# Order of transposes and one-hot products in the attention edge pass

## The chip, the cores and the metric

The program runs on one core of one Trainium2 chip. The metric is the device time of one execution in microseconds. The kernel before took 4116.12 us in the median of three runs (4115.34 to 4116.28).

## The reference, cut to what matters

Two graph attention layers over 3125 nodes and 100,000 edges sorted by target, then a sum over neighbours and three dense layers, each part closed by a layer norm:

```python
def gatv2_layer(x, src, dst, Wl, Wr, att, bias, n_nodes, heads):
    xl = (x @ Wl).reshape(N, heads, Dh)
    xr = (x @ Wr).reshape(N, heads, Dh)
    e = leaky_relu(xl[src] + xr[dst], 0.2)
    logits = einsum('ehd,hd->eh', e, att)
    m = segment_max(logits, dst)
    a = exp(logits - m[dst])
    alpha = a / segment_sum(a, dst)[dst]
    out = segment_sum(alpha[:, :, None] * xl[src], dst)
    return out.mean(axis=1) + bias
```

The first layer has 8 heads, the second 4; a head has 64 features.

## The kernel before, in words

The edges are laid out in 900 units of 125 edges (`T`). A chunk is 20 units, so there are 45 chunks a layer (`NCH`); a chunk is worked in five turns `q` of four units each (`Q`). `edge_pass` (line 753) is one pass over the 45 chunks; it runs once for each attention layer, so there are 450 turns.

For its four units a turn needs a matrix of 128 rows and 500 columns: rows 0 to 63 are the features of the source nodes, rows 64 to 127 those of the target nodes, one column for each edge. `turn(c, q)` (line 876) makes it in one PSUM bank, `ps_x`:

- Four transposes (line 887), one a unit: `xs` holds the gathered source rows, 125 edges by 64 features in float32, and the identity is the moving operand. They write PSUM partitions 0 to 63.
- Four products (line 890), one a unit: a bfloat16 table `xw` of the window's node features (96 by 64) against a one-hot matrix `oht` (96 by 125). They write PSUM partitions 64 to 127. The last one counts up the semaphore `x_ready`, on which ScalarE waits to copy the bank to SBUF (`copy_xT`, line 988), to be used by TensorE one turn later.

TensorE's order is written out by hand in `body` (line 959), chunk by chunk and turn by turn: `turn`; then four parts in which the projection of the turn before (`project`, line 900, 500 moving columns in float32, all 128 rows and columns of the array; four in layer 1, two in layer 2) alternates with the weighted sums of a unit three chunks back (`sums`, line 951); then `reduce` of three turns back (lines 909 and 912), whose small matmuls write four strips of 32 PSUM partitions; and in turns 0, 1 and 2 a group of full-array transposes and matmuls to `ps_t` (lines 922, 930 to 933, 940). So the turns 1, 2 and 3 start behind such a full-array group, the turns 0 and 4 behind `reduce`. A float32 matmul that is no transpose stands as two instructions in the profile (line 900 has x2 where one is written), a transpose as one.

GpSimd gathers the source rows, one indirect DMA for each unit (line 825), into a ring of 6 chunks in layer 1 and 9 in layer 2, and may refill a chunk's tile when `sums` has used it (`v_ready`, line 822). TensorE waits for a chunk's 20 gathers at its turn 0 (line 879).

Of the kernel before, what the change touches and what calls it, by code (L numbers as in the profile page):

```python
# [14 lines left out]
N, D, E = 3125, 64, 100000  # L15
# [3 lines left out]
T = 125  # L19
# [3 lines left out]
Q = 4  # L23
# [20 lines left out]
NQ = 5  # L44
# [123 lines left out]
def sbuf(nc, ctx, name, shape, dt=F32):  # L168
    return ctx.enter_context(nc.sbuf_tensor(name, shape, dt))
# [583 lines left out]
def edge_pass(nc, k, lay):  # L753
# [12 lines left out]
    with ExitStack() as ctx:  # L766
        ph, nm = "e_", lay.nm + "e_"
        dlb = [sbuf(nc, ctx, f"{nm}dlb{r}", [3 * WN, CU * T], BF16) for r in range(3)]
        oht = [sbuf(nc, ctx, f"{nm}oht{r}", [3 * WN, CU * T], BF16) for r in range(2)]
# [30 lines left out]
        xs, gath = lay.xs, lay.gath  # L800
        xw, wins, ld_x, ld_w = lay.xw, lay.wins, lay.ld_x, lay.ld_w
# [15 lines left out]
        with nc.Block() as block:  # L817
# [57 lines left out]
            def _(pe):  # L875
                def turn(c, q):
                    r = c.slot(XR)
                    if q == 0:
                        pe.wait_ge(gath[r], c.uses(XR) * GB)
                        pe.wait_ge(ld_x[c.slot(3)], c.uses(3) * 16 * CU)  # L880
                        pe.wait_ge(s["oht_ready"], c.val(1, 1))
                    if c.after(1) or q >= 2:
                        pe.wait_ge(s["xT_ready"], c.val(NQ, q - 1))
                    ps = ps_x[(c.slot(2) * NQ + q) % 2]
                    for j in range(Q):
                        n = j * NQ + q
                        pe.transpose(ps[0:D, j * T:(j + 1) * T], xs[r][:, n, 0:D], k.ident[0:T, 0:T])  # L887
                    for j in range(Q):
                        n = j * NQ + q
                        ins = pe.matmul(ps[D:128, j * T:(j + 1) * T], xw[c.slot(3)][:, n, :],  # L890
                                        oht[c.slot(2)][:, n * T:(n + 1) * T], start=True, stop=True)
                    ins.then_inc(s["x_ready"], 1)

                def project(c, q, part):
# [64 lines left out]
                def body(c, q):  # L959
                    if c.there():  # L960
                        turn(c, q)
                    zc, zq = lag(c, q, 1)
                    bc, bq = lag(c, q, 15)
                    rc, rq = lag(c, q, 3)
                    for part in range(4):
                        if part % (4 // C) == 0 and (c.after(1) or q >= 1) and zc.there():
                            project(zc, zq, part // (4 // C))
                        if c.after(3) and bc.there():
                            sums(bc, bq, part)
                    if (c.after(1) or q >= 3) and rc.there():  # L970
                        reduce(rc, rq)
                    b = c.back(2)
                    if c.after(2) and b.there():
                        if q == 0:
                            maxima_out(b)
                        if q == 1:
                            fifth_out(b)
                        if q == 2:
                            weights_out(b)
# [1076 lines left out]
```

## Time and profile before

| | |
|---|---|
| median of three runs | 4116.12 us |
| profiled execution, its own time | 4112.72 us |
| its span on the chip | 4110.9 us |
| TensorE (PE) busy | 3302.8 us, 80% |
| GpSimd (POOL) busy | 2883.6 us, 70% |
| VectorE (DVE) busy | 2788.8 us, 68% |
| ScalarE (ACT) busy | 1702.9 us, 41% |
| mean granted clock of TensorE | 0.896 |

In the profile L900 is line 900 of the kernel; PE is a matmul, PEld the weight load ahead of it. The edge pass of layer 1 lies at about 190 to 1790 us, that of layer 2 at about 2110 to 3470 us. Ends of matmuls are modelled, so the start times say more than the busy times: the time from the start of one matmul to the start of the next is what a matmul costs in a stream. A group that stands in one row as x4 gives its first start and the time to its modelled last end; the start of its last matmul is that end less the duration of one.

### The profile page before, as it was taken

How to read it: one execution, taken by the hardware profiler on the slowest of the kernel's cores; microseconds unless marked ns; L12 is line 12 of the kernel's file. 1: busy time of each engine (PE TensorE's matmuls, PEld its weight loads, DVE VectorE, ACT ScalarE, POOL GpSimd, SP SyncE). 2: the span in 40 equal slices, each digit the busy share in tenths (PEclk: the TensorE clock that was granted, in tenths of full speed). 3: DMA queues.
4: the chain of work that ended last, by engine and by line, in shares of the span. 5: the costliest groups of instructions: out<-in, count | busy, mean ns of one | idle time of the engine just before them, and what ended most of it. 6: DMA issues, size and time to landing. Idle time of an engine off the chain costs nothing. (4 is left out here: it accounts for less than half of the span.)

```text
span 4110.9 us, 76192 instructions
## 1 busy us (share of the span) xinstructions
PE 3302.8 (80%) x24219; PEld 2216.7 (54%) x24219; DVE 2788.8 (68%) x6704; ACT 1702.9 (41%) x3682; POOL 2883.6 (70%) x2229
## 2 busy tenths in 40 slices
PE   0499999999999999986259977777777778457886
PEld 0246666666666666664226645554555546345663
DVE  3558888888888888875527855556555666378872
ACT  3254444444444444412215433333333332156651
POOL 4488888887777777434778888888888883567860
PEclk9999999999999999966679988888888887589897
DMA  2233334343333333222124433333333332112120
GB/s 57 51 67 86 84 83 87 85 87 85 87 84 87 85 85 81 68 59 65 49 42 84 92 67 68 73 67 69 67 72 70 68 68 45 35 34 47 40 46 28
DMA packets 612700, 277.98 MB, mean 68 GB/s; under 512 B 450601, under 2 KB 572877, under 8 KB 611716
## 3 DMA queue, kind: packets, MB, share of 16 engines
q1 hardware_dynamic: 263920, 103.06, 11.5%
q0 software_dynamic: 110784, 80.17, 11.1%
q10 hardware_dynamic: 237600, 89.88, 9.0%
q8 instruction: 198, 3.24, 0.3%
q14 instruction: 198, 1.62, 0.1%
HBM read 164.01 MB, written 106.40 MB: 66 GB/s over the span
## 5 line engine op out<-in xcount | busy, mean ns | idle before, releaser
L900 PE MATMUL L_e_ps_z<-L_e_xT,L_w_abs 128*128 128x500 f32 x2700 | 1496.6, 640 | 0.0
L825 POOL DMA_INDIRECT L_e_xs<-in_x_dram,src_idx x880 | 1185.3, 1347 | 343.9 <-issue 261.0
L825 POOL DMA_INDIRECT L_e_xs<-x_d,src_idx x820 | 1071.2, 1306 | 253.3 <-issue 249.8
L951 PEld LDWEIGHTS L_e_ps_v<-L_e_xs,L_e_p 125*128 125x128 f32 x5400 | 857.2, 203 | 628.1 <-issue 571.6
L995 ACT ACTIVATE L_e_rl<-L_e_ps_z 128x500 f32<-128x500 f32 x1350 | 793.0, 587 | 877.8 <-PE L_e_ps_z L900 877.8
L951 PE MATMUL L_e_ps_v<-L_e_xs,L_e_p 125*128 125x65 f32 x5400 | 793.9, 274 | 12.1 <-DVE L_e_acc L1179 10.4
L1179 DVE SCALAR_TENSOR_TENSOR L_e_acc<-L_e_acc,L_e_row,L_e_ps_v 128x130 f32<-128x130 f32 (+1 forms) x1440 | 448.3, 311 | 426.7 <-PE L_e_ps_v L951 283.1
L887 PE MATMUL L_e_ps_x<-ident,L_e_xs 125*64 125x125 f32 x1800 | 288.1, 285 | 301.5 <-DMA L_e_xs<-x_d,src_idx 245.2
L988 ACT ACTIVATE L_e_xT<-L_e_ps_x 128x500 f32<-128x500 f32 x450 | 264.2, 587 | 610.5 <-PE L_e_ps_x L890 603.8
L900 PEld LDWEIGHTS L_e_ps_z<-L_e_xT,L_w_abs 128*128 128x128 f32 x2700 | 425.7, 197 | 76.2 <-issue 22.4
L1162 DVE TENSOR_TENSOR L_e_p<-L_e_ohc,L_e_ae 125x640 f32<-125x640 f32 x540 | 427.1, 818 | 0.0
L1652 POOL DMA_INDIRECT g_xs<-x_d,src_idx x240 | 295.8, 1233 | 132.9 <-issue 72.5
L887 PEld LDWEIGHTS L_e_ps_x<-ident,L_e_xs 125*64 125x64 f32 x1800 | 188.6, 119 | 345.1 <-DMA L_e_xs<-x_d,src_idx 254.4
L1184 DVE SCALAR_TENSOR_TENSOR L_e_acc<-L_e_acc,L_e_keep,L_e_ps_v 128x65 f32<-128x65 f32 x540 | 134.9, 277 | 304.4 <-PE L_e_ps_v L951 302.3
L1090 DVE SCALAR_TENSOR_TENSOR L_e_f<-L_e_rl,L_sign 128x500 f32<-128x500 f32 x450 | 326.1, 725 | 21.1 <-ACT L_e_rl L995 20.9
L1090 DVE SCALAR_TENSOR_TENSOR L_e_f<-L_e_rl,L_sign,L_e_f 128x500 f32<-128x500 f32 x450 | 330.1, 734 | 4.1 <-ACT L_e_rl L995 0.6
L1768 ACT ACTIVATE g_cnt<-g_ps_c 125x400 bf16<-125x400 f32 x480 | 241.6, 504 | 127.9 <-PE g_ps_c L1703 122.1
L1799 DVE TENSOR_SCALAR g_ohk<-t_keys_n,t_key_of 125x200 bf16<-125x200 bf16 x960 | 225.6, 330 | 7.5 <-PE g_ps_c L1703 7.1
L909 PE MATMUL L_e_ps_l<-L_e_xT,L_w_lin 128*32 128x125 f32 x3600 | 190.3, 283 | 14.1 <-DVE L_e_f L1090 14.1
L1703 PE MATMUL g_ps_c<-g_ohk,g_ohr 125*128 125x200 bf16 x960 | 169.6, 264 | 36.6 <-DVE g_ohk L1799 34.3
L1713 PE MATMUL g_ps_s<-g_x,g_cnt 125*128 125x192 bf16 x1500 | 194.7, 258 | 0.2 <-DVE g_sums L1805 0.2
L890 PE MATMUL L_e_ps_x<-L_e_oht,L_e_xw 96*64 96x125 bf16 x1800 | 192.8, 232 | 0.0
(304 smaller groups left out, 3661.0 us busy)
## 6 DMA issues: line engine op xcount, KB each, us to landing
L_v_d<-L_e_acc ACTq DMA_DIRECT2D x225, 260.0 KB
L_e_dlb<-dloc_d SPq DMA_DIRECT2D x90, 468.8 KB
L_v_d<-L_e_acc ACTq DMA_DIRECT2D x225, 130.0 KB
L_e_xw<-x_d SPq DMA_DIRECT2D x1800, 12.0 KB
L_e_xs<-in_x_dram,src_idx POOLq DMA_INDIRECT x900
L_e_xs<-x_d,src_idx POOLq DMA_INDIRECT x900
L_e_lim<-limits_d SPq DMA_DIRECT2D x180, 39.1 KB
g_xs<-x_d,src_idx POOLq DMA_INDIRECT x240, 3.0
```

The costliest lines, as they stand in the source:

```text
L825: pool.indirect_dma_start(xs[c.slot(XR)][:, n, 0:D], None, lay.x_rows, bass.IndirectOffsetOnAxis(k.src_idx[:, u:u + 1], 0)).then_inc(gath[ ...
L887: pe.transpose(ps[0:D, j * T:(j + 1) * T], xs[r][:, n, 0:D], k.ident[0:T, 0:T])
L900: pe.matmul(ps_z[part % ZR][:, 0:QT], lay.w_abs[:, part * 128:(part + 1) * 128], xT[q][:], start=True, stop=True).then_inc(s["z_ready"], 1)
L951: ins = pe.matmul(ps_v[u // 2 % 2][:, u % 2 * VX + v * XW:u % 2 * VX + (v + 1) * XW], p[st % 3][:, u % NQ, v, :, :].rearrange("e n h -> e ...
L988: act.activation(xT[q][:], ps_x[(c.slot(2) * NQ + q) % 2][:, 0:QT], ACT.Copy).then_inc(s["xT_ready"], 1)
L995: act.activation(rl[n % NE][:], ps_z[part % ZR][:, 0:QT], ACT.Relu, scale=1.0 - SLOPE).then_inc(s["relu_done"], 1)
L1090: dve.scalar_tensor_tensor(out=f[g % 3][:], in0=rl[(C * g + part) % NE][:], scalar=lay.sign[:, part:part + 1], in1=rl[(C * g) % NE][:] if ...
L1162: ins = dve.tensor_tensor(p[n % 3][:, :, v, :, :], ohc[c.slot(2)][:, us, :].unsqueeze(3).to_broadcast([T, NQ, WN, HL]), ae[c.slot(2)][:, u ...
L1179: ins = dve.scalar_tensor_tensor(out=to, in0=prev, scalar=row[c.slot(2)][:, u:u + 1], in1=ps_v[u // 2 % 2][:, u % 2 * VX:(u % 2 + 1) * VX] ...
L1652: pool.indirect_dma_start(xs[p][:, j, :], None, table, bass.IndirectOffsetOnAxis(k.src_idx[:, u:u + 1], 0)).then_inc(gath[p], 16)
L1768: act.activation(cnt[i % CR][:, :, 2 * j:2 * j + 2, :], ps_c[n % 2][0:T, 0:2 * KEYS].rearrange("r (u t n) -> r t u n", u=2, n=EN), ACT.Cop ...
L1799: dve.tensor_scalar(ohk[v % KR][:], keys_n[:], key_of[:, v:v + 1], None, ALU.is_equal).then_inc(s["hot"], 1)
```

## The change

In `turn`, each unit's product is issued first and its transpose right behind it, through the four units. The operands, the outputs and the number of instructions are the same. The count on `x_ready` moves from the last product to the last transpose, which is now the last instruction.

```diff
                     for j in range(Q):
                         n = j * NQ + q
-                        pe.transpose(ps[0:D, j * T:(j + 1) * T], xs[r][:, n, 0:D], k.ident[0:T, 0:T])
-                    for j in range(Q):
-                        n = j * NQ + q
-                        ins = pe.matmul(ps[D:128, j * T:(j + 1) * T], xw[c.slot(3)][:, n, :],
-                                        oht[c.slot(2)][:, n * T:(n + 1) * T], start=True, stop=True)
+                        pe.matmul(ps[D:128, j * T:(j + 1) * T], xw[c.slot(3)][:, n, :],
+                                  oht[c.slot(2)][:, n * T:(n + 1) * T], start=True, stop=True)
+                        ins = pe.transpose(ps[0:D, j * T:(j + 1) * T], xs[r][:, n, 0:D], k.ident[0:T, 0:T])
                     ins.then_inc(s["x_ready"], 1)
```

## Rows read from the trace of the kernel before

**Rows 1.** The page: busy time by engine, and PE and its clock in 40 slices.

```profile
PE 3302.8 (80%) x24219; PEld 2216.7 (54%) x24219; DVE 2788.8 (68%) x6704; ACT 1702.9 (41%) x3682; POOL 2883.6 (70%) x2229
...
PE   0499999999999999986259977777777778457886
...
PEclk9999999999999999966679988888888887589897
```

**Rows 2.** Busy time of each engine in a stretch of layer 1 and of layer 2.

```profile
core 0: us, PE busy (x) PEld busy (x) DVE busy (x) ACT busy (x) POOL busy (x), PEclk, DMA share, GB/s
300.00:1400.00 1100.00, 1100.00 (x7902) 730.63 (x7894) 918.26 (x1958) 543.21 (x1122) 868.68 (x642) 1.00 0.39 86
2400.00:3400.00 1000.00, 779.30 (x5966) 511.32 (x5965) 579.81 (x1396) 357.75 (x808) 809.99 (x624) 0.87 0.36 69
```

**Rows 3.** Groups of PE instructions, 300 to 1400 us: busy, mean ns, idle before.

```profile
L887 PE MATMUL L_e_ps_x<-ident,L_e_xs 125*64 125x125 f32 x624 | 93.9, 273 | 0.0
```

**Rows 4.** Waits (total us, times, longest): POOL in 900 to 1400 us.

```profile
POOL L_e_xs L825 <- PE L_e_ps_v L951: 39.9, 13, 3.8
```

**Rows 5.** Waits: PE in 190 to 300 us, the start of layer 1.

```profile
PE L_e_ps_x L887 <- DMA L_e_xs<-in_x_dram,src_idx: 6.8, 1, 6.8
```

**Rows 6.** Waits: PE in 2400 to 3400 us, layer 2.

```profile
PE L_e_ps_x L887 <- DMA L_e_xs<-x_d,src_idx: 220.7, 31, 8.2
```

**Rows 7.** PE in order of time (start, us to last end): layer 1, behind a full-array group.

```profile
1000.65 0.70 PE L922 MATMUL L_e_ps_t<-ident,L_e_mx 128*125 128x128 f32 x4
1001.19 0.59 PE L887 MATMUL L_e_ps_x<-ident,L_e_xs 125*64 125x125 f32 x4
1001.71 0.41 PE L890 MATMUL L_e_ps_x<-L_e_oht,L_e_xw 96*64 96x125 bf16 x4
1002.05 1.10 PE L900 MATMUL L_e_ps_z<-L_e_xT,L_w_abs 128*128 128x500 f32 x2
1003.00 0.56 PE L951 MATMUL L_e_ps_v<-L_e_xs,L_e_p 125*128 125x65 f32 x4
1003.39 1.06 PE L900 MATMUL L_e_ps_z<-L_e_xT,L_w_abs 128*128 128x500 f32 x2
1004.28 0.56 PE L951 MATMUL L_e_ps_v<-L_e_xs,L_e_p 125*128 125x65 f32 x4
```

**Rows 8.** The same turn in narrow windows: transposes 2 to 4, transpose 4, product 4.

```profile
1001.30 0.48 PE L887 MATMUL L_e_ps_x<-ident,L_e_xs 125*64 125x125 f32 x3
...
1001.51 0.27 PE L887 MATMUL L_e_ps_x<-ident,L_e_xs 125*64 125x125 f32 x1
...
1001.91 0.22 PE L890 MATMUL L_e_ps_x<-L_e_oht,L_e_xw 96*64 96x125 bf16 x1
```

**Rows 9.** PE in order of time: layer 1, a turn that starts behind `reduce`.

```profile
1022.00 0.42 PE L909 MATMUL L_e_ps_l<-L_e_xT,L_w_lin 128*32 128x125 f32 x8
1022.24 0.40 PE L912 MATMUL L_e_ps_l<-L_e_f,L_sign_sum 128*32 128x125 f32 x8
1022.56 0.62 PE L887 MATMUL L_e_ps_x<-ident,L_e_xs 125*64 125x125 f32 x4
1023.11 0.41 PE L890 MATMUL L_e_ps_x<-L_e_oht,L_e_xw 96*64 96x125 bf16 x4
```

**Rows 10.** PE in order of time: neighbour sums, both on the full array.

```profile
3679.88 0.25 PE L1703 MATMUL g_ps_c<-g_ohk,g_ohr 125*128 125x200 bf16 x1
3679.96 1.02 PE L1731 MATMUL g_ps_w<-g_blk,g_winhot 96*98 96x512 f32 x2
```

**Rows 11.** PE in order of time: merge, full-array transposes, then matmuls to 64 partitions.

```profile
1887.10 0.65 PE L1373 MATMUL L_n_ps_t<-ident,L_n_agg 125*128 125x125 f32 x4
1887.67 1.07 PE L1392 MATMUL L_n_ps_o<-L_n_aggT,L_n_wl 128*64 128x125 f32 x8
```

**Rows 12.** Stretches again: early layer 2, merge, all of layer 1 (columns of Rows 2).

```profile
2190.00:2350.00 160.00, 159.18 (x1369) 105.64 (x1368) 132.43 (x323) 81.67 (x185) 130.10 (x99) 1.00 0.48 91
1880.00:2100.00 220.00, 97.83 (x558) 77.00 (x557) 106.92 (x173) 42.87 (x102) 131.35 (x114) 0.65 0.17 43
262.00:1787.00 1525.00, 1521.92 (x10926) 1007.27 (x10925) 1267.89 (x2698) 754.14 (x1557) 1126.13 (x834) 1.00 0.37 83
```

## The prediction

> **What bounds the kernel now.** I read the page's totals and slices first, then the busy time by stretch, the waits, and last the order of time of single turns. PE is the busiest engine, and its slices say where: nines through layer 1, sevens through most of layer 2 [rows 1]. A busy share is no proof, so the waits decide.
>
> In layer 1 PE is busy for all of the 1100 us looked at, at a granted clock of 1.00 [rows 2], and its transposes there have an idle time before them of 0.0 [rows 3]. It is GpSimd that waits for PE there, to have a tile of the ring back [rows 4]. So PE's own stream sets the time of layer 1, and what a turn gets longer, the layer gets longer. Only at its start does PE wait once for a gather, 6.8 us [rows 5]; that was for chunk 2, so what chunks 0 and 1 lose is taken out of that wait. 43 chunks, 215 turns, count in full.
>
> In layer 2 PE waits 31 times in 1000 us, 220.7 us in all, for the gathers of a chunk, once a chunk [rows 6]. So there GpSimd and its gathers set the time: a chunk takes 1000 / 31 = 32.3 us, of which PE waits 7.1 us. What a chunk of PE's work gets longer is taken from that wait while it stays under 7.1 us. The first ten chunks of layer 2, whose rows were partly gathered ahead, run without waits (PE 159.18 of 160 us busy [rows 12]); time lost there only makes PE reach the waiting part later, with the waits of 35 chunks to make it good.
>
> **What a switch costs.** Call a transpose T, a product P, the first projection Z, the first matmul of the sums V. In the turn of [rows 7, 8]:
>
> - T to T: 1001.30 to 1001.51 in two steps, 0.107 us each.
> - T4 to P1: 1001.51 to 1001.71, 0.20 us. So 0.09 us more than a T takes in its stream.
> - P1 to P4: 1001.71 to 1001.91, 0.20 us, three steps. A P in its stream takes less than 0.06 us; the first step is some 0.08 us, since P1's weights weren't loaded ahead.
> - P4 to Z1: 1001.91 to 1002.05, 0.145 us; again 0.09 us over the 0.055 that P takes.
> - Z1 to V: 0.95 us (1002.05 to 1003.00), where the next pair, whose weights could be loaded ahead during other work, takes 0.89 us (1003.39 to 1004.28).
>
> So twice a turn, between T and P and between P and Z, the stream stops for about 0.09 us, and the matmul behind the stop shows its weight load: 0.025 us for P. For T it is seen in the turn behind `reduce`: T1 to P1 is 0.55 us there [rows 9] against 0.52 us in [rows 7], so 0.03 us.
>
> What makes a switch? Three pairs of rows tell. A bfloat16 matmul followed by a float32 one, both on the full array, has no stop: 0.08 us for 200 columns [rows 10]. So the data type isn't it. The full-array transposes of L922 are followed by our T without one: the last starts at 1001.35 - 0.27 = 1001.08, T1 at 1001.19, 0.11 us [rows 7]. But L912, which writes strips of 32 partitions, followed by T has one: 1022.37 to 1022.56, 0.19 to 0.20 us [rows 9], and so have full-array transposes followed by float32 matmuls into 64 partitions: 1887.48 to 1887.67 [rows 11]. So T goes with the full array though it fills only 64 columns, P goes with the matmuls that use a part of the columns, and each change between the two kinds costs a stop. In the old order a turn has two such changes (T to P, P to Z), and a third before T1 when `reduce` was ahead. In the new order it has eight: into P1, and seven between T and P. T4 to Z1 is none.
>
> The Trainium skill says so as a rule, in "TensorEngine Tiling (Array Packing)", Key Properties: a change of the tiling mode drains TensorE, a change of tile within a mode doesn't; its Gotcha 2 adds that column tiling and the transpose mode for float32 input exclude each other. The trace agrees with both.
>
> **The change part by part.** Nothing is added or removed: the same eight matmuls and weight loads, no DMA, no wait. Only their order, in 450 turns. I sum from the start of the last matmul ahead of the turn to the start of V.
>
> Before: behind `reduce` (turns 0 and 4) 1022.37 to V; with T1 at 0.20, T1 to P1 0.55, P1 to Z1 0.34, Z1 to V 0.94, that is 2.03 us. Behind a full-array group (turns 1 to 3): 1001.08 to 1003.00 = 1.92 us [rows 7, 9].
>
> After, in both kinds of turn:
>
> - into P1: 0.20 us. A stop is due there in every turn. From `reduce` to P the trace has no row; both kinds use a part of the columns, but of another width. Bounds: 0.10 (no stop) to 0.20. I take 0.20, as for every other change of shape seen; by the lower one turns 0 and 4 lose 0.10 less, 9 us over the layer.
> - P to T, four times: 0.145 as from P to Z, and 0.025 of load shown behind the stop: 0.17, together 0.68. No row has P to T. Bounds: 0.055, a P in its stream with no stop, and 0.145 + 0.107 = 0.25, the stop and as much again as a whole T. I take 0.17, the nearest row, since L912 to T is a stop too.
> - T to P, three times: 0.20 + 0.03 of T's own load = 0.23, together 0.69 (0.68 unrounded).
> - T4 to Z1: 0.107 + 0.03 = 0.13 us.
> - Z1 to V: no stop ahead of Z1, so its load runs beside T4. 0.94 less the load that showed, twice the 0.05 by which it exceeds the next pair: 0.84 us.
>
> Sum 0.20 + 0.68 + 0.68 + 0.13 + 0.84 = 2.53 us. Turns 0 and 4 lose 0.50, turns 1 to 3 lose 0.61; mean 0.57 us a turn, 2.8 us a chunk.
>
> Layer 1: 215 x 0.57 = 122 us, all on the path. Layer 2: 2.8 us of the 7.1 us that PE waits a chunk, hidden by the gathers; only the last chunk, behind its last gather, has nothing to hide it: 3 us. If the cover weren't there the layer would pay 225 x 0.57 = 128 us. The clock there is 0.87 and some turns run at the lower level, where a stop may cost more; even at twice the price, 5.7 us, it stays under 7.1.
>
> `x_ready` now comes from T4, whose modelled duration is 0.27 us where that of P4 is 0.22 [rows 8]. ScalarE's copy starts 0.05 us later against its last matmul; the copy is used by Z in the next turn, some 5 us on, so this costs nothing, and 0.05 us a turn (11 us) if that cover were gone. The same count lets SP load and VectorE build the one-hot tiles of chunks ahead, also far off.
>
> Sum: 4112.7 us (the profiled execution) + 122 + 3 = 4238 us. The median of the runs stands 3.4 us above that execution, so 4241 us; I say 4242.
>
> **The rivals.**
>
> *The pairs overlap (faster).* T writes PSUM partitions 0 to 63 and P 64 to 127, different columns of the array. For it: L909's eight matmuls of 125 columns in four strips take from 1022.00 to 1022.24, four side by side in the time of one [rows 9]. If T and P were tiles of one mode, P would lie beside T: 0.20 + 0.03 + 3 x 0.107 + 0.20 + 0.94 = 1.69 us, 0.34 less behind `reduce`, 0.23 less behind a full-array group, mean 0.27; 215 turns give -59 us, 4057 us. Against it: T4 to P1 stops already now, though P's columns are free. The condition from which it decides is that this stop is not the shape but only the first use of the other columns. The Trainium skill's rule that different tiles can load and multiply in parallel (same page, Key Properties) would give this result. Chance 6%. A weaker form, in which stops vanish but nothing overlaps, saves about 0.1 us a turn, some 4090 us; 3%.
>
> *P to T is free.* Stops only on the way into P. Then 4 x 0.115 less: 0.11 us a turn, +24 us, 4140 us. Against it: P to Z and L912 to T both stop. 5%.
>
> *The clock falls or layer 2 loses its cover.* The stops make PE do less in a turn. In the merge, with many stops and waits, the granted clock is 0.65; in early layer 2, with 4.5 us turns and the two stops, it is 1.00 [rows 12]. A new layer 1 turn loses 8 stops of 0.09 in over 7.5 us, nearer to the latter. If layer 1 fell to layer 2's 0.87, between the levels of 1.2 and 2.4 GHz, it would take 1525 / 0.87 - 1525 = 228 us more, 4470 us. If layer 2 lost a third of its cover, some 40 us more, 4280 us. 5% together.
>
> *It makes no difference*, because PE's stream isn't what sets layer 1 after all, 4116 us: against it stands the zero wait. 2%.
>
> **How the numbers follow.** The forecast has 79%, and its own bounds, from the P-to-T bounds and the entry from `reduce`, are 4140 (which is the second rival) to 4310 (0.25 instead of 0.17, four times, 215 turns: +69). I don't give these ends full weight: 4175 to 4290 leaves out the fast rivals, the free P to T and the fallen clock, some 20% with the edges. Within 0.2%, about 8 us, is what can't be told from no change: 3%. Faster 9%, slower 88%.
>
> **What would show it.** In the order of time of a layer 1 turn T and P should stand singly, P to T 0.17 us apart and T to P 0.23, with an idle time in the weight loads before each; Z1 should follow T4 without one. A turn should be 0.5 to 0.6 us longer in layer 1 at a clock of 1.00, GpSimd should wait longer for PE there, and in layer 2 PE should wait some 4 us a chunk where it waits 7, the period of 32.3 us unchanged. I am wrong if T and P start within 0.03 us of each other, if P to T is 0.06, or if layer 2 is longer by over 10 us.

## The result, and the profile after

The changed kernel takes 4258.53 us in the median of four runs, where the kernel before takes 4116.13: a ratio of 1.0345, interval 1.0327 to 1.0363, or 142 us more. The profiled execution took 4257.54 us, with a span of 4255.7 us.

The forecast was 4242 us, slower, by a stop of TensorE's stream at each change between transpose (T) and product (P). That is what the trace shows. First the page, busy time by engine and PE's slices:

```profile
PE 3554.1 (84%) x24219; PEld 2298.5 (54%) x24219; DVE 2794.7 (66%) x6704; ACT 1701.6 (40%) x3682; POOL 2894.6 (68%) x2229
...
PE   0499999999999999996619998888888888557786
```

As many instructions as before, yet PE is "busy" for 251 us more [rows 1]. The modelled durations, 0.24 and 0.30 us in the rows below, reach over the 0.17 and 0.23 us to the next start, the stop included. So a stop counts as busy time, and the busy time says nothing of work.

A turn of layer 1 of the changed kernel, PE in order of time (start, us to the last end; the answer to [rows 7]). Line 887 is now the product and line 889 the transpose; 898 is the projection (its first one is Z1) and 949 the weighted sums (V):

```profile
1002.39 0.40 PE L910 MATMUL L_e_ps_l<-L_e_f,L_sign_sum 128*32 128x125 f32 x8
1002.72 0.70 PE L938 MATMUL L_e_ps_t<-ident,L_e_lg 128*125 128x128 f32 x4
1003.35 0.24 PE L887 MATMUL L_e_ps_x<-L_e_oht,L_e_xw 96*64 96x125 bf16 x1
1003.53 0.30 PE L889 MATMUL L_e_ps_x<-ident,L_e_xs 125*64 125x125 f32 x1
1003.75 0.24 PE L887 MATMUL L_e_ps_x<-L_e_oht,L_e_xw 96*64 96x125 bf16 x1
1003.93 0.30 PE L889 MATMUL L_e_ps_x<-ident,L_e_xs 125*64 125x125 f32 x1
...
1004.56 0.24 PE L887 MATMUL L_e_ps_x<-L_e_oht,L_e_xw 96*64 96x125 bf16 x1
1004.73 0.30 PE L889 MATMUL L_e_ps_x<-ident,L_e_xs 125*64 125x125 f32 x1
1004.87 1.01 PE L898 MATMUL L_e_ps_z<-L_e_xT,L_w_abs 128*128 128x500 f32 x2
1005.71 0.56 PE L949 MATMUL L_e_ps_v<-L_e_xs,L_e_p 125*128 125x65 f32 x4
```

From start to start P to T is 0.17 to 0.18 us, T to P 0.23, T4 to Z1 0.14, Z1 to V 0.84. From the last transpose of the group ahead (1003.42 - 0.27 = 1003.15) to P1 it is 0.20. The sum to V is 2.56 us; 2.53 was forecast, 1.92 was the old.

The busy time by stretch (the answer to [rows 2 and 12]: layer 1, and a stretch of layer 2 as far into it as before), the waits of POOL in 900 to 1400 us, of PE in 190 to 300 us, and of PE in 2500 to 3560 us (the answers to [rows 4 to 6]):

```profile
300.00:1400.00 1100.00, 1100.00 (x7282) 703.07 (x7281) 848.62 (x1804) 501.34 (x1033) 795.55 (x591) 1.00 0.37 79
2530.00:3530.00 1000.00, 851.40 (x5962) 527.46 (x5962) 582.37 (x1402) 357.18 (x808) 812.15 (x617) 0.91 0.35 69
...
262.00:1914.00 1652.00, 1649.22 (x10927) 1050.57 (x10925) 1270.64 (x2697) 754.53 (x1557) 1120.87 (x834) 1.00 0.35 76
```

```profile
POOL L_e_xs L825 <- PE L_e_ps_v L949: 73.7, 13, 5.8
```

```profile
PE L_e_ps_x L887 <- DMA L_e_xs<-in_x_dram,src_idx: 3.1, 1, 3.1
```

```profile
PE L_e_ps_x L887 <- DMA L_e_xs<-x_d,src_idx: 154.5, 31, 6.2
```

In 1100 us of layer 1 PE now gets through 7282 matmuls instead of 7902, still at a clock of 1.00 and still with no wait. GpSimd waits 5.7 us a chunk for PE where it waited 3.1. In layer 2 PE's wait falls from 7.1 to 5.0 us a chunk.

Where the time lies shows in the first and last start of the transposes of each layer (duration min/median/max in ns, then first and last start in us), before and after:

```profile
L887 PE MATMUL L_e_ps_x<-ident,L_e_xs x900: 267/270/417, 198.8 to 1766.1; 125*64 125x125 f32 x180
L887 PE MATMUL L_e_ps_x<-ident,L_e_xs x900: 267/270/418, 2112.8 to 3448.1; 125*64 125x125 f32 x180
```

```profile
L889 PE MATMUL L_e_ps_x<-ident,L_e_xs x900: 295/297/418, 198.7 to 1893.9; 125*64 125x125 f32 x180
L889 PE MATMUL L_e_ps_x<-ident,L_e_xs x900: 295/297/418, 2240.1 to 3593.0; 125*64 125x125 f32 x180
```

Layer 1 is 1695.2 us long instead of 1567.3, 127.9 more. The start of layer 2 moves by 127.3 us, its last transpose by 144.9: layer 2 is 17.6 us longer, where 3 were forecast.

So two questions are left for experiments. Is it the change of array shape that costs, and not the mix of types or the order? And where do the 15 us in layer 2 come from that the forecast doesn't have?

### The profile page after: what moved, and what is told of

The parts are those of the page before. It is cut to its first block and busy times, and to the rows that moved or that the text cites. A ratio compares the mean times of both kernels' runs of the same rounds, so it can differ in the third digit from the quotient of the medians.

```text
span 4255.7 us, 76192 instructions
## 1 busy us (share of the span) xinstructions
PE 3554.1 (84%) x24219; PEld 2298.5 (54%) x24219; DVE 2794.7 (66%) x6704; ACT 1701.6 (40%) x3682; POOL 2894.6 (68%) x2229
## 5 line engine op out<-in xcount | busy, mean ns | idle before, releaser
L898 PE MATMUL L_e_ps_z<-L_e_xT,L_w_abs 128*128 128x500 f32 x2700 | 1438.4, 618 | 0.0
L825 POOL DMA_INDIRECT L_e_xs<-x_d,src_idx x820 | 1086.5, 1325 | 253.3 <-issue 249.5
L887 PE MATMUL L_e_ps_x<-L_e_oht,L_e_xw 96*64 96x125 bf16 x1800 | 446.7, 248 | 210.2 <-DMA L_e_xs<-x_d,src_idx 158.8
L889 PE MATMUL L_e_ps_x<-ident,L_e_xs 125*64 125x125 f32 x1800 | 551.9, 307 | 0.0
L898 PEld LDWEIGHTS L_e_ps_z<-L_e_xT,L_w_abs 128*128 128x128 f32 x2700 | 438.2, 202 | 33.2 <-issue 16.8
L887 PEld LDWEIGHTS L_e_ps_x<-L_e_oht,L_e_xw 96*64 96x64 bf16 x1800 | 193.9, 108 | 444.7 <-DMA L_e_xs<-x_d,src_idx 167.3
L889 PEld LDWEIGHTS L_e_ps_x<-ident,L_e_xs 125*64 125x64 f32 x1800 | 200.1, 111 | 126.9
```

The costliest lines, as they stand in the source:

```text
L825: pool.indirect_dma_start(xs[c.slot(XR)][:, n, 0:D], None, lay.x_rows, bass.IndirectOffsetOnAxis(k.src_idx[:, u:u + 1], 0)).then_inc(gath[ ...
L889: ins = pe.transpose(ps[0:D, j * T:(j + 1) * T], xs[r][:, n, 0:D], k.ident[0:T, 0:T])
L898: pe.matmul(ps_z[part % ZR][:, 0:QT], lay.w_abs[:, part * 128:(part + 1) * 128], xT[q][:], start=True, stop=True).then_inc(s["z_ready"], 1)
```

## The experiments

Twelve runs, in three groups of four, each group on another chip and with its own runs of the kernel before. These took 4147, 4121 and 4113 us, so each run is held against its own group. The first group has no trace of the kernel before. "Layer 1" and "layer 2" below are spans between the first and the last projection (line 900, 898 in the changed kernel) of a layer in the profiled execution, and are held against the first profile; there the kernel before has 1575.1 and 1338.6 us, the changed one 1701.2 and 1353.8.

**Products first.** Four products, then four transposes.

```diff
-  T0 T1 T2 T3 P0 P1 P2 P3
+  P0 P1 P2 P3 T0 T1 T2 T3
```

> The four products of a turn first, then its four transposes; all else as in the kernel before. Theory S (each change between matmuls that use a part of the columns and those on the full array stops the stream for 0.09 us, and the next weight load shows): changes per turn go from 2 (3 behind reduce) to 2 (1 behind reduce, if strips of 32 to 64 columns is no change). Sum from the last matmul ahead to V: 0.20 + 0.20 + 0.145 + 0.35 + 0.11 + 0.84 = 1.85 us against 2.03 and 1.92, mean -0.12 us a turn, layer 1 -26 us, about 4090 us. Rival A (it is the nearness of products and transposes, or the product going first, that costs): no gain or slower, 4116 us or more.

Measured: ratio 0.9903, interval 0.9871 to 0.9934, or -41 us where -26 were expected. In order of time, layer 1:

```profile
1002.99 0.70 PE L940 MATMUL L_e_ps_t<-ident,L_e_lg 128*125 128x128 f32 x4
1003.62 0.41 PE L888 MATMUL L_e_ps_x<-L_e_oht,L_e_xw 96*64 96x125 bf16 x4
1003.96 0.62 PE L891 MATMUL L_e_ps_x<-ident,L_e_xs 125*64 125x125 f32 x4
1004.41 1.01 PE L900 MATMUL L_e_ps_z<-L_e_xT,L_w_abs 128*128 128x500 f32 x2
1005.26 0.56 PE L951 MATMUL L_e_ps_v<-L_e_xs,L_e_p 125*128 125x65 f32 x4
```

From the last matmul ahead (1003.69 - 0.27) to V 1.84 us; 1.85 was expected. A chunk takes 34.76 us through most of layer 1, where the kernel before takes 35.39: 0.126 us a turn less, 0.12 expected. Layer 1 is 17 us shorter in the profiled execution; a third of its chunks took about 35.3 us. The kernel before was slow on this chip as well, so the 41 us can't be told apart into order and chip, and the size is taken from the rows. The product going first costs nothing, so that half of Rival A is out. Its other half, that a product next to a transpose costs, is for the next runs.

**Two and two.** P0 P1 T0 T1 P2 P3 T2 T3: four changes.

> Two products, two transposes, two products, two transposes. Theory S: four changes a turn between old 2 and new 8; sum 2.07 us a turn against 2.03 and 1.92, mean +0.10 us, layer 1 +22 us, layer 2 a few us: 4135 to 4145 us. Rival A (a cost for each product that stands next to a transpose): two of the four pairs are neighbours in order, so half of the 142 us, 4187 us.

Measured: ratio 1.0146, interval 1.0103 to 1.0189, that is +61 us, close to the rival and outside the 4135 to 4145 us (19 to 29 more) of the switch theory. But the excess isn't between products and transposes. Ahead of its projections in layer 1 PE had 31.3 us of "issue" waits, where the products-first kernel had 3.4, and VectorE had "remote" waits ahead of its sums, where the kernel waits for the store of an earlier sum; the kernel before had none of these. Waits in 300 to 1700 us:

```profile
PE L_e_ps_z L900 <- issue: 31.3, 29, 4.8
```

```profile
DVE L_e_acc L1184 <- remote: 65.0, 24, 3.9
```

The run was therefore made again in another group.

> Two products, two transposes, twice, once more, because the first run of it was on a chip where VectorE and ScalarE also waited for stores in layer 1. Switch theory: 35.9 us a chunk in layer 1, +22 us there, +20 to +35 us in all with what layer 2 adds. Rival A (half of the full cost): +70 us.

Measured: ratio 1.0041, interval 1.0028 to 1.0055, +17 us. PE has no wait in layer 1 now:

```profile
1004.64 0.30 PE L888 MATMUL L_e_ps_x<-L_e_oht,L_e_xw 96*64 96x125 bf16 x2
1004.87 0.40 PE L891 MATMUL L_e_ps_x<-ident,L_e_xs 125*64 125x125 f32 x2
1005.20 0.30 PE L888 MATMUL L_e_ps_x<-L_e_oht,L_e_xw 96*64 96x125 bf16 x2
1005.43 0.41 PE L891 MATMUL L_e_ps_x<-ident,L_e_xs 125*64 125x125 f32 x2
1005.67 1.01 PE L900 MATMUL L_e_ps_z<-L_e_xT,L_w_abs 128*128 128x500 f32 x2
```

A chunk takes 35.95 us in every chunk from the fourth on (35.9 expected), layer 1 1599.0 us, +24. The total is below the expected 20 to 35 because layer 2 is 12 us shorter than before. Rival A wanted 70, so it is out. The steps between the matmuls are the same in both runs (P to T 0.15 us, T to P 0.20), so the other 44 us of the first run are not the price of this order. They went with the waits shown; why that execution had them is not known.

**Wide products.** The shape is the only thing taken out. The window table is given 128 columns with zeros in the first 64, and the product writes all 128 partitions; the transpose then writes over the lower half. Types, order and the transpose mode stay those of the changed kernel.

```diff
-    lay.xw = [sbuf(nc, ctx, f"{lay.nm}e_xw{r}", [3 * WN, CU, D], BF16) for r in range(3)]
+    lay.xw = [sbuf(nc, ctx, f"{lay.nm}e_xw{r}", [3 * WN, CU, 128], BF16) for r in range(3)]
...
+                    pool.memset(lay.xw[r][:, :, 0:D], 0.0).then_inc(s["ones"], 1)
...
-                        pe.matmul(ps[D:128, j * T:(j + 1) * T], xw[c.slot(3)][:, n, :],
+                        pe.matmul(ps[0:128, j * T:(j + 1) * T], xw[c.slot(3)][:, n, :],
```

> The order of the changed kernel, product then transpose through the four units, but each product on the full array: its stationary operand is 128 columns wide, the first 64 zeros, so it writes zeros to PSUM partitions 0 to 63, which the transpose behind it overwrites. Theory S: no change of shape within a turn, so no stop: layer 1 turns 0.31 us shorter than before, -67 us, about 4050 us. Rival B (the stop comes with the change between bfloat16 product and float32 transpose, whatever columns they use): stays at about 4258 us.

> The same wide products, all four ahead of the four transposes. Theory S: as the wide pairs, about 4050 us, since order no longer matters. Rival B: two stops a turn left, about 4090 us, well below the wide pairs.

Measured: ratios 0.9899 (0.9866 to 0.9931) for the pairs and 0.9885 (0.9841 to 0.9928) with the products first, against a kernel before of 4147 us: 4101 and 4102 us. That is 46 and 44 us less where 67 were expected; Rival B, which had the pairs at 4258, is far off. The pairs were run again:

> The wide products in pairs once more, for its size: layer 1 chunks of 33.9 us where the kernel before has 35.4, less the waits for gathers that now show in layer 1: -45 to -60 us in all, layer 2 within 15 us of the old.

Measured: 4085.52 us, ratio 0.9934, interval 0.9921 to 0.9947, -27 us. In order of time, a turn behind `reduce` that had waited for its gather:

```profile
1006.77 0.23 PE L890 MATMUL L_e_ps_x<-L_e_oht,L_e_xw 96*128 96x125 bf16 x1 [0.96 <-DMA L_e_xs<-in_x_dram,src_idx]
1006.84 0.27 PE L893 MATMUL L_e_ps_x<-ident,L_e_xs 125*64 125x125 f32 x1
1006.95 0.22 PE L890 MATMUL L_e_ps_x<-L_e_oht,L_e_xw 96*128 96x125 bf16 x1
1007.01 0.27 PE L893 MATMUL L_e_ps_x<-ident,L_e_xs 125*64 125x125 f32 x1
...
1007.45 1.00 PE L902 MATMUL L_e_ps_z<-L_e_xT,L_w_abs 128*128 128x500 f32 x2
```

P to T is 0.06 and T to P 0.11 us, in the very order that costs 0.17 and 0.23 when the product fills half the columns. A bfloat16 product next to a float32 transpose is no stop: Rival B is out, and the price belongs to the shape. The edit also moves the product's first PSUM partition from 64 to 0. [rows 11] speak against this being what counts: line 1392 writes 64 partitions from partition 0 on, and a stop stands ahead of it. An undisturbed chunk is 33.89 us (expected 33.9) in pairs and 33.82 with the products first: order no longer matters, within 0.014 us a turn.

The gain is smaller than the expected 45 to 60 us, for two reasons seen in the trace. Layer 1 is 39 us shorter, not 64, as it has caught up with its gathers: PE waits for them 7 times, 14.4 us, in 300 to 1700 us, and those chunks take 34.9 to 39.8 us, 19 us more than seven undisturbed ones. And layer 2 came out 15 us longer. Which leads to the second question.

**One layer at a time.** The pair order in one layer, the old order in the other. `PAIRS` and `OLD` stand here for the two orders, which the kernels write out; `lay.norm` is true in layer 2.

```diff
-                    for what, j in PAIRS:
+                    for what, j in (OLD if lay.norm else PAIRS):     # the other kernel: the reverse
```

> The pair order in layer 1 alone. Switch theory: the whole of the 127 us measured between the starts of layer 1 and layer 2 stays, chunks of 38.35 us; layer 2 within 20 us of the old. +115 to +145 us. Rival (layer 2 carries a share of its own): the two halves don't add up to 142 us.

> The pair order in layer 2 alone. Switch theory with full cover by the gathers: +3 us. What the changed kernel showed: +17 us in layer 2. If those came from the order, +10 to +20 us here; if they hung on layer 1's end, +3 us.

Beside them, the kernel before itself, for its trace:

> The kernel before, unchanged, for its trace on this chip: layer 1 chunks of 35.4 us, layer 2 chunks of 32.1 us, the 820 gathers of layer 2 busy for some 1070 us. If layer 1 chunks are longer or uneven, the difference belongs to the chip and not to an edit.

Measured: layer 1 alone 1.0287 (1.0265 to 1.0310), +118 us; layer 2 alone 1.0046 (1.0030 to 1.0063), +19 us by the ratio. Together 137 of the 142. By the traces layer 1 is +121 against the kernel before in the same group (1697.9 against 1576.7) and layer 2 +15 (1356.1 against 1341.1). So layer 2's share is real, it needs nothing from layer 1, and it is not the 3 us of the last chunk.

The gathers say where it is. GpSimd issues them one behind the other with 0.30 us between, and in 2230 to 3600 us of the changed kernel it waits for almost nothing else, so their own durations set their pace. The 820 gathers of layer 2 (busy time of line 825 or its equivalent from 2050 us to the end of the layer; columns: window, length, POOL busy, clock, DMA share, GB/s). Kernel before:

```profile
2050.00:3650.00 1600.00, 1071.25 (x820) 0.84 0.33 64
```

Changed kernel:

```profile
2050.00:3650.00 1600.00, 1086.46 (x820) 0.87 0.33 64
```

The pair order in layer 2 alone:

```profile
2050.00:3650.00 1600.00, 1088.16 (x820) 0.86 0.33 64
```

They became 15.2 us longer in the changed kernel, as much as the layer. All the runs agree (us; layer 2 and gathers against the kernel before at 1338.6 and 1071.25):

| kernel | layer 2 | gathers busy |
|---|---|---|
| before, again | +2.5 | +1.9 |
| changed | +15.2 | +15.2 |
| products first | +1.4 | +2.4 |
| two and two / again | -3.5 / -12.2 | -3.0 / -11.2 |
| wide pairs / again | +2.5 / +14.8 | +4.2 / +15.6 |
| wide, products first | +22.0 | +24.1 |
| pairs in layer 1 only | +2.4 | +2.0 |
| pairs in layer 2 only | +17.5 | +16.9 |

The same program has been 12 us apart in two executions on two chips (wide pairs). And the sign doesn't follow the stops: the wide products, with none inside a turn, have the longest layer 2 of all.

**Filler.** PE's chunk made as much longer without any change of shape.

```diff
+                    for j in range(Q if lay.norm else 0):
+                        n = j * NQ + q
+                        pe.transpose(ps[0:D, j * T:(j + 1) * T], xs[r][:, n, 0:D], k.ident[0:T, 0:T])
+                    if lay.norm:
+                        pe.transpose(ps[0:D, 0:T], xs[r][:, q, 0:D], k.ident[0:T, 0:T])
```

> The old order, but in layer 2 each turn first issues five extra transposes (the four of the turn and the first again) into the same place: 5 x 0.107 = 0.54 us of PE work with no change of shape. Switch theory: 2.7 us a chunk, hidden by the gathers. Theory G (a longer PE chunk moves VectorE's work against the gathers, and the layer's length changes by what the gathers' own busy time changes): anything from -15 to +25 us, equal to the change of the gathers' busy time within 3 us, as the other order shows. Rival (switches themselves slow layer 2): within 3 us of before while the pair order in layer 2 is 10 to 20 us slower.

Measured: ratio 1.0018, interval 1.0009 to 1.0028, +7 us; layer 2 +6.7 and its gathers +7.0 against the kernel before of the first profile, +4.2 and +5.1 against that of the group. PE's wait went to 129.9 us in the stretch in which the pairs in layer 2 have 132.8, so the same cover was used up. Theory G's relation holds; the rival would want 3 us at the most, which 4.2 doesn't clearly refute. Nor is the +7 us of the whole clean: in the profiled execution layer 1, which the edit doesn't touch, was 9.6 us longer as well. So this run alone doesn't decide between the two.

**VectorE's part.** Why does a gather take longer? A gather's instruction on GpSimd takes 1.20 to 1.22 us when no VectorE operation overlaps it, in all fourteen executions (223 to 269 of the 820). At 1.21 us the 820 would take 992 us; the kernel before has 79 us over that, the changed one 94. In the changed kernel, layer 2, next to the weights' product (line 1160, 1162 in the kernel before) and the operation that spreads the one-hot matrix (line 1068, 1070 before):

```profile
2606.05 1.21 POOL L825 DMA_INDIRECT L_e_xs<-x_d,src_idx  x1 [0.30 <-issue]
2607.56 1.88 POOL L825 DMA_INDIRECT L_e_xs<-x_d,src_idx  x1 [0.31 <-issue]
2609.75 1.38 POOL L825 DMA_INDIRECT L_e_xs<-x_d,src_idx  x1 [0.30 <-issue]
```

```profile
2607.54 0.82 DVE L1160 TENSOR_TENSOR L_e_p<-L_e_ohc,L_e_ae 125x640 f32<-125x640 f32 x1
...
2608.79 1.27 DVE L1068 TENSOR_SCALAR L_e_oht<-L_e_dlb,L_oht_node 96x2500 bf16<-96x2500 bf16 x1
```

And once in the kernel before, where it fell well:

```profile
2636.58 1.21 POOL L825 DMA_INDIRECT L_e_xs<-x_d,src_idx  x1 [0.30 <-issue]
```

```profile
2636.55 0.87 DVE L1070 TENSOR_SCALAR L_e_oht<-L_e_dlb,L_oht_node 96x2500 bf16<-96x2500 bf16 x1
```

The gather at 2607.56 starts while line 1160 runs and takes 1.88 us; the spread comes up during that gather and takes 1.27 us for 0.87; the gather at 2609.75 starts while the spread runs and takes 1.38. In the kernel before gather and spread start within 0.03 us of each other, and neither is held up.

Line 1160 shows the rule best. Over all fourteen executions 1395 gathers start while it runs (0.02 us or more behind its start, 0.13 or more ahead of its end), and every one of them ends 1.07 to 1.10 us after it does: here 2608.36 and 2609.44. So such a gather is held until the operation has ended. It is these that grew. In the kernel before there are 93, 21 us over 1.21 each; in the changed one 131, 47 us; with the pairs in layer 2 alone 43 us, and with the fillers, which change no shape, 39 us. In the other runs they are 15 to 22 us. What the other gathers lose went down by 11 us in the changed kernel and in the filler run. So a longer PE chunk, whatever makes it longer, puts line 1160 where more of it falls on the starts of gathers. The wide products have 15 to 19 us of theirs here and lose the rest beside other operations.

The spread was taken as the operation to test:

```diff
-                    dve.tensor_scalar(oht[c.slot(2)][:], dlb[c.slot(3)][:], lay.oht_node[0:3 * WN, :], None,
+                    w = 8 if lay.norm and c.after(2) else CU * T
+                    dve.tensor_scalar(oht[c.slot(2)][:, 0:w], dlb[c.slot(3)][:, 0:w], lay.oht_node[0:3 * WN, :], None,
```

> The old order; in layer 2, from chunk 2 on, VectorE's operation that spreads the one-hot matrix (line 1070, 2500 columns, 0.87 us, once a chunk) does 8 columns only, so the matrix is that of an earlier chunk and layer 2's result is another. Theory G (layer 2 is as long as its gathers' busy time makes it, and a gather is held up by VectorE operations such as this one): 37 of the operations overlap gathers by some 35 us with about half of it added to the gathers, so busy time and layer 2 both shorter by 10 to 20 us. Rival (the gathers' busy time varies for another reason): no change beyond 3 us, since VectorE is idle for 40% of layer 2.

Measured: ratio 0.9913, interval 0.9899 to 0.9927. Layer 2 takes 1305.9 us, 32.7 less, and its gathers:

```profile
2050.00:3650.00 1600.00, 1037.31 (x820) 0.83 0.33 65
```

33.9 us less than before, up to three times what was expected. So VectorE, with 40% to spare, does bear on the length of this layer. But most of the 34 us are not the spread's own: gathers that it touches were 14 us over 1.21 each before and are 7 now, and all the others went from 66 to 39. And the short spread still takes 0.62 us in the median. What it changed above all is where the operations behind it fall.

> The old order; in layer 2 the same VectorE operation runs twice a chunk, the second behind the first. Theory G: gathers' busy time and layer 2 both longer by 10 to 20 us. Rival: no change beyond 3 us; 0.9 us a chunk is covered on VectorE.

Measured: ratio 1.0005, interval 0.9995 to 1.0014: a miss. Layer 2 +5.7 us, gathers +6.5 in the profiled execution: the two still go together, but a second spread right behind the first hardly costs more. Taking the first away shifts everything behind it on VectorE as well, and so does adding one, so neither is a clean price of the operation.

The Trainium skill, "SBUF — State Buffer", Who interferes with whom, has such a rule: VectorE in a two-port mode, which a `tensor_scalar` can enter, and GpSimd exclude each other from a shared pair of ports, whichever issues first keeping it for the whole instruction. The rows above agree in that both engines were held up. No run here showed which mode the spread was in. By the page's other rule a VectorE instruction with two inputs from SBUF contends with a GpSimd instruction that reads SBUF. Line 1160 has two such inputs, and the 1395 gathers held behind it agree; no run varied its inputs.

## Why the prediction was right

**What bounds layer 1: right.** No wait of PE before or after, the clock at 1.00 in both, and a chunk of 38.35 us against 35.39: +0.59 us a turn where 0.57 was forecast. The later chunks repeat to 0.01 us.

**What a switch costs: right.** The medians over all turns are P to T 0.174 us (0.17 forecast, from rows that had no such step), T to P 0.227 (0.23), T4 to Z1 0.134 (0.13), into P1 0.200 behind `reduce` and 0.202 behind full-array transposes (0.20). The open bound, whether strips of 32 partitions followed by a product into 64 stop too, is settled: they do. The wide products show that it is the shape.

**Which turns count: right.** Chunks 0 and 1 were to be paid by the wait of 6.8 us [rows 5], and they were: chunk 2 starts at 256.67 us where it started at 256.59. The wait itself only fell to 3.1, as another one ahead of it, 3.4 us of PE for VectorE at line 909, is gone as well. Layer 1 came to 126 to 128 us, where the sum had 122; the difference is 0.02 us a turn, 215 times.

**Layer 2 hidden but for 3 us: the step that failed.** The prediction said that it would be wrong if layer 2 grew by over 10 us, and it grew by 15 to 18. The cover held: PE still waits 5.0 us a chunk, and the last chunk's turns cost 1.7 us, not 3. What failed was the unsaid assumption that the gathers' own pace would stay the same. The layer's length follows its gathers, and these are held up when they start beside some of VectorE's operations, line 1160 above all; a PE chunk of another length puts these elsewhere. That the stops themselves add nothing beyond this is not shown: the fillers, a PE chunk as long without them, cost 4 to 7 us and the pairs 15 to 17, and the same program differed by 12 us between two chips. "The period of 32.3 us unchanged" was the wrong sentence: over the whole layer a chunk of gathers takes 0.37 us more, 41 times.

**The copy starts 0.05 us later: not seen.** It is hidden, as layer 1 is accounted for without it.

**The rivals.** Overlap in separate columns: no, T and P never start within 0.17 us of each other. P to T free: no, 0.17. The clock: 1.00 in layer 1, and in layer 2 it rose from 0.87 to 0.91, where PE's waits are shorter; more stops did not lower it.

The sum by stage: 127 to 128 us in layer 1 and 15 to 18 in layer 2, against 142.4 between the medians. In the profiled executions it is 144.8. The forecast stayed 16 us short of the measured time; 5 of them are the steps of layer 1, the rest is layer 2, and no error hid another.

## What to carry to other kernels

Group small matmuls by the part of the array's columns they use before anything else. Each crossing cost 0.09 us of stopped stream plus the weight load that can no longer run ahead, and a product padded with zeros to the full width was cheaper than a narrow one, in both orders tried. Where a layer waits for GpSimd's gathers, slack on PE covers PE's own work, but a change of rhythm still moves VectorE against the gathers: hold 1 to 2% of such a stage as uncertain, and compare the gathers' busy time before the matmuls'. Then look for the VectorE operation beside which the long gathers start.

## What the runs showed of the hardware that was not expected

A narrow float32 transpose (125 by 64) goes with the full array and not with the other 64-column tiles, and it costs no stop behind a full-array one. The gathers of 820 units differ by up to 58 us in busy time between kernels with the same transfers (1037.3 to 1095.3 us), and the layer's length follows that number to within 2.1 us in all thirteen other executions. A wide product, with twice the weight columns, takes no more of the stream than a narrow one: 0.055 us from one to the next in the median, where the narrow took 0.057. And a gather that starts while the two-input float32 operation of line 1160 runs ends 1.07 to 1.10 us after it, in 1395 of 1395 cases.
